# Graph convolution: one-bin tiles in the edge table (500 for 588), and four bin additions a group spread over VectorE's step

## The chip, the cores and the metric

The kernel runs on one core of a Trainium2 chip. The metric is the device time of one execution in microseconds, the median of 3 runs. Engines are named as the profile names them: PE is TensorE (PEld its weight loads), DVE is VectorE, ACT is ScalarE, POOL is GpSimd, SP is SyncE.

## What is computed

A graph of 3750 nodes with 256 features and 60000 edges goes through four layers, each added to its input: a relational attention, a mixture of small experts, a graph convolution (`_L1_gnn_ref`), and a routed mixture of 16 experts. The change concerns the third:

```python
row, col = (ei[0], ei[1])
filt = jax.nn.silu(rbf @ Wf1 + bf1) @ Wf2 + bf2     # rbf: 60000 x 20, Wf1: 20 x 256, Wf2: 256 x 256
msg = x[col] * filt
agg = jax.ops.segment_sum(msg, row, num_segments=x.shape[0])
h = jax.nn.silu(agg @ Wu1 + bu1) @ Wu2 + bu2
# then a batch norm of h over the nodes, and x + bn
```

`row` is the edge's `src` and `col` its `dst`. So for each edge a filter of 256 values is computed from 20 attributes, multiplied by the gathered row of the `dst` node, and summed into the `src` node.

## The kernel before

**Bins and tiles.** The 3750 nodes are 30 bins of 128 (`NT`). Edges are sorted by the bin of the node that they are summed into, and cut into tiles of 128 edges, one edge to a partition. K = 4 tiles make a group. `rank` (L407) computes for each edge its place in the order; it rounds the edges of a bin up to `SIZE = group * P` places. For the table of the convolution (`table1`, records of 24 floats: 20 attributes, the `dst` row, the place of `src` in its bin) `group` is K, so each bin is padded to a multiple of 512 places, and the four tiles of a group belong to one bin. The table has ET = 588 tiles, 147 groups. It is first filled with empty records, whose row number is 0 and whose place is -1 (`fill1`, L1953, in 28 DMAs), then POOL scatters the real records into it beside the attention stage and elsewhere. The bin of each group is in `bins1`. The attention stage has a table of its own, by `dst`, in the same 588 tiles.

**The convolution (`convolve`, L1331)** is one stage between two barriers. SP loads the first 588 tiles of `table1` into SBUF in one DMA (L1384), then the smaller weights. Then all engines walk the same steps t = 0 to 151; in a step each works on groups at different distances behind t (`parts`). Steps 0 to 5 and 147 to 151 are written out, the rest is a loop of three steps. In step t:

- POOL gathers 4 x 128 rows of `xtab` for a group, three slots `got`, released by the messages of the group three earlier (L1399).
- ACT copies attributes to bf16 (L1415), applies silu to the first layer (L1420), moves transposed attributes out of PSUM (L1424).
- PE, in this order: four transposes of the attributes of group t-1 into `pT` (L1439); the first layer of group t-2 into `p1` (L1446); the second layer of group t-3 into `pf[0]` and `pf[1]`, two tiles each (L1454); the sum over the edges of group t-4, four matmuls with the one-hot matrix that accumulate in 256 columns of one of three banks `psum` (L1463).
- DVE, in this order: the number of the bin of group t-5 is read from SBUF into a register (`value_load`, L1481); the one-hot of group t-3 (L1486); three instructions that split the attributes of group t into a high and a low bf16 part, `rest`, copy and low part (L1492, L1494, L1496; the last lets PE transpose that group in the next step); the bias added to both halves of the filter of group t-3 (L1502); both halves of the messages (L1507); `agg[bin] += psum` for group t-5 (L1512).

The semaphores that matter below: `filtered` (PE to DVE, a half of `pf` is done), `filt_ready` and `msg_ready` (DVE, halves of the filter and of the messages), `attr_ready` (DVE to PE, the low part is written), `summed` (PE to DVE), `agg_done` (DVE to PE, the bank may be written again). `filt` has one buffer, `msg`, one-hot, `attr` and `got` have three. In the attention stage DVE reads a bin number in the same way: of its four maxima in a row (L863, each released by PE) the fourth has such a load ahead of it. A matmul with fp32 operands appears in the profile as two records.

```python
if 5 in parts:
    dve.wait_ge(summed, t - 4)
    wait_positive(dve, agg_done, t - 5)
    at = flat(agg[:, bass.ds(bin5, 1), :])
    v.tensor_tensor(at, at, psum[s5][:, 0:D], ALU.add).then_inc(agg_done, 1)
```

## Time and profile before

| what | value |
|---|---|
| median of 3 runs | 4170.98 us (4170.66 to 4171.43) |
| the profiled execution: its time, its span | 4176.44 us, 4174.7 us |
| PE busy | 2928.3 us, 70% of the span |
| DVE busy | 2177.3 us, 52% |
| POOL busy | 2277.2 us, 55% |
| ACT busy | 1210.5 us, 29% |
| the convolution, from its first DMA to its last addition | 2398.2 to 3301.6 us |

The stages follow one another with a barrier between them, so a stage's length goes whole into the total. A share of the whole span is an average over stages with different limits; the stage in question has to be read by itself. "Idle before" in a row names what ended the wait. A row of the timeline with xN merges N instructions that follow each other; their ends overlap the next start a little, so the distance of two starts (the pitch) is shorter than a duration.

### The profile page before, as it was taken

What the parts mean: (1) busy time and instruction counts of PE and PEld (TensorE: products, weight loads), DVE (VectorE), ACT (ScalarE), POOL (GpSimd) and SP (SyncE); (2) the same over time, 40 slices, a digit from 0 to 9 for tenths busy, and PEclk for the clock granted to TensorE, in tenths of its full rate; (3) what the DMA queues carried; (4) which work ended last, traced back from release to release, by engine and by line L of the source; (5) the groups of instructions that cost most, each with busy time, mean ns of one, the idle gap of its engine ahead of it and who ended that gap; (6) DMA issues with size and microseconds to landing.
All of it is one profiled execution on the core that took longest, in us unless ns stands there. A gap on an engine that the chain in (4) does not pass through costs nothing. (4 is left out here: it accounts for less than half of the span.)

```text
span 4174.7 us, 73619 instructions
## 1 busy us (share of the span) xinstructions
PE 2928.3 (70%) x20296; PEld 2364.7 (57%) x20297; DVE 2177.3 (52%) x5961; ACT 1210.5 (29%) x3266; POOL 2277.2 (55%) x2336
## 2 busy tenths in 40 slices
PE   5199101777777777776379679999999864299990
PEld 1188101555555555555255358888888633288990
DVE  8411002877777777777743557777777444011112
ACT  1123000444444444444223223333333231022220
POOL 2777775777777777777240056666666200511115
PEclk8599655998998999999679789999999875599995
DMA  3344101222222222225100143333335501155533
GB/s 105 108 135 137 40 2 32 63 65 63 63 64 63 64 64 63 64 64 62 23 19 1 47 136 89 90 89 90 90 90 84 52 0 39 49 175 173 171 104 114
DMA packets 209214, 317.71 MB, mean 76 GB/s; under 512 B 63367, under 2 KB 150063, under 8 KB 208388
## 3 DMA queue, kind: packets, MB, share of 16 engines
q0 software_dynamic: 95008, 179.89, 19.9%
q1 hardware_dynamic: 103204, 127.24, 9.4%
q10 hardware_dynamic: 10944, 9.97, 0.7%
q8 instruction: 17, 0.28, 0.0%
q14 instruction: 41, 0.34, 0.0%
HBM read 248.03 MB, written 68.84 MB: 76 GB/s over the span
## 5 line engine op out<-in xcount | busy, mean ns | idle before, releaser
L1402 POOL DMA_INDIRECT conv_got<-xtab,conv_rowidx x588 | 565.8, 962 | 313.2 <-DVE conv_msg L1507 156.6
L806 POOL DMA_INDIRECT att_got<-feat,att_rowidx x588 | 573.2, 975 | 201.5 <-issue 150.2
L294 POOL DMA_INDIRECT table<-l0a_rec,l0a_addr x469 | 458.2, 977 | 216.7 <-issue 146.1
L1454 PE MATMUL conv_pf<-conv_wf,conv_act 128*128 128x256 f32 x2352 | 534.0, 380 | 0.2 <-DVE conv_filt L1502 0.2
L812 POOL DMA_INDIRECT table<-recs_rec,recs_addr x432 | 423.2, 980 | 131.6 <-issue 130.4
L1454 PEld LDWEIGHTS conv_pf<-conv_wf,conv_act 128*128 128x128 f32 x2352 | 447.6, 190 | 76.9 <-issue 0.8
L982 PE MATMUL att_pmax<-all_identb,att_away 128*128 128x512 bf16 x588 | 261.1, 444 | 203.9 <-DVE att_elo L901 203.2
L863 DVE TENSOR_REDUCE att_tmax<-att_pmax 128x4 f32<-128x512 f32 x588 | 373.8, 680 | 31.1 <-PE att_pmax L986 27.6
L986 PE MATMUL att_pmax<-all_identb,att_ehi 128*128 128x128 bf16 x2352 | 383.6, 242 | 0.0
L986 PE MATMUL att_pmax<-all_identb,att_elo 128*128 128x128 bf16 x2352 | 383.3, 242 | 0.0
L1420 ACT ACTIVATE conv_act<-conv_p,conv_bf 128x512 f32<-128x512 f32 x294 | 186.2, 684 | 552.1 <-PE conv_p L1446 552.1
L1502 DVE TENSOR_TENSOR conv_filt<-conv_pf,conv_bf 128x512 f32<-128x512 f32 x294 | 202.8, 691 | 222.1 <-PE conv_pf L1454 222.1
L986 PEld LDWEIGHTS att_pmax<-all_identb,att_elo 128*128 128x128 bf16 x2352 | 260.5, 111 | 93.0 <-issue 41.6
L1013 PE MATMUL att_psum<-att_f,att_onehot 128*128 128x260 f32 x1176 | 303.7, 403 | 1.9 <-DVE att_f L925 1.9
L1873 DVE TENSOR_TENSOR moe_hid<-moe_gatev,moe_p 128x512 f32<-128x512 f32 x76 | 52.2, 687 | 484.4 <-ACT moe_gatev L1853 484.4
L1825 PE MATMUL moe_p<-moe_xT,moe_w 128*128 128x128 f32 x2432 | 287.5, 277 | 17.4 <-issue 7.1
L957 ACT ACTIVATE att_f<-att_got,att_ex 128x64 f32<-128x64 f32 x1176 | 294.5, 333 | 0.0
L1825 PEld LDWEIGHTS moe_p<-moe_xT,moe_w 128*128 128x128 f32 x2432 | 278.7, 193 | 23.5 <-issue 18.3
L1463 PE MATMUL conv_psum<-conv_msg,conv_onehot 128*128 128x256 f32 x1176 | 279.0, 380 | 5.6 <-DVE conv_msg L1507 5.6
L1788 POOL DMA_INDIRECT moe_got<-xtab,moe_tokens x76 | 72.0, 948 | 368.2 <-PE moe_pT L1814 358.6
L706 PE MATMUL proj_ps<-proj_w,proj_xs 128*128 128x260 f32 x960 | 220.1, 388 | 74.6 <-DVE proj_wr L652 70.0
L986 PEld LDWEIGHTS att_pmax<-all_identb,att_ehi 128*128 128x128 bf16 x2352 | 260.0, 111 | 0.0
(336 smaller groups left out, 5074.0 us busy)
## 6 DMA issues: line engine op xcount, KB each, us to landing
moe_w<-in_L_ffn_w SPq DMA_DIRECT2D x96, 512.0 KB
feat<-proj_out SPq DMA_DIRECT2D x30, 1040.0 KB
results<-moe_y ACTq DMA_DIRECT2D x76, 128.0 KB, 1.7
att_got<-feat,att_rowidx POOLq DMA_INDIRECT x588
conv_got<-xtab,conv_rowidx POOLq DMA_INDIRECT x588, 2.8
xtab<-ln_row SPq DMA_DIRECT2D x60, 128.0 KB, 1.7
table<-l0a_rec,l0a_addr POOLq DMA_INDIRECT x469
table<-recs_rec,recs_addr POOLq DMA_INDIRECT x469, 2.1
```

What stands on the lines that cost most here:

```text
L294: self.nc.gpsimd.indirect_dma_start(out=self.table, out_offset=bass.IndirectOffsetOnAxis(ap=self.addrs[:, j:j + 1], axis=0), in_=self.recs ...
L806: nc.gpsimd.indirect_dma_start(out=got[g % 3][:, k, :], out_offset=None, in_=feat, in_offset=bass.IndirectOffsetOnAxis(ap=rowidx[:, g * K ...
L812: nc.gpsimd.indirect_dma_start(out=table1, out_offset=bass.IndirectOffsetOnAxis(ap=addr1[:, i:i + 1], axis=0), in_=rec1[:, i, :], in_offse ...
L863: count(v.tensor_reduce(tmax[:, k, :], pmax[k][:, :, :], AX.X, ALU.max))
L957: nc.scalar.activation(f[s2][:, k, h, 0:HD], got[s2][:, k, h * HD:(h + 1) * HD], ACT.Copy, scale=ex[:, k, h:h + 1]).then_inc(last_ready, 1)
L982: nc.tensor.matmul(pmax[k][:, :, :], away[s1][:, k, :], bcast(c["identb"][:, :], [[0, HEADS], [1, P]]), start=True, stop=False, skip_group ...
L986: ins = nc.tensor.matmul(pmax[k][:, h, :], part[s1][:, k, h:h + 1].broadcast_to([P, P]), c["identb"][:, :], start=False, stop=(part is elo ...
L1013: ins = nc.tensor.matmul(psum[:, 0:HEADS * H1], oh[s2][:, k, :], flat(f[s2][:, k, :, :]), start=(k == 0), stop=(k == K - 1))
L1402: nc.gpsimd.indirect_dma_start(out=got[g % 3][:, k, :], out_offset=None, in_=xtab, in_offset=bass.IndirectOffsetOnAxis(ap=rowidx[:, g * K ...
L1454: ins = nc.tensor.matmul(pf[b][:, k, :], act1[s3][:, h, (2 * b + k) * P:(2 * b + k + 1) * P], wf2[:, h, :], start=(h == 0), stop=(h == 1))
L1463: ins = nc.tensor.matmul(psum[s4][:, 0:D], oh[s4][:, k, :], msg[s4][:, k, :], start=(k == 0), stop=(k == K - 1))
L1825: ins = nc.tensor.matmul(ps[w][:, j * P:(j + 1) * P], wt[w][:, k, j * P:(j + 1) * P], xT[w][:, k, :], start=(k == 0), stop=(k == 1))
```

## The change

Three parts. (1) `table1` has tiles of one bin each: `rank` by `src` rounds to 128 places instead of 512, the table has ET1 = 500 tiles (125 groups), and `bins1` holds the bin of each tile. A group of four tiles may now span two bins. (2) Since the four tiles of a group no longer share a bin, PE keeps their sums apart: two tiles write the two halves of one bank, the other two those of the next, and the three banks turn by half groups. (3) DVE adds four sums a group instead of one, each with its own bin number. The additions of group t-5, k = 0 to 3, are spread over the step, and the split of the attributes is spread too. The steps written out at the end are now 7 instead of 5 (the loop takes 123 of 125 groups). The empty records are written in 25 DMAs of 20 tiles instead of 28 of 21.

```diff
+ET1 = 500
+TS1 = ET1 + -(-EJ // P)
...
-TABLE1_PARTS = 28
+TABLE1_PARTS = 25
...
-        rank(nc, "by_src", c, Bins(nc, k, "src", src, src_loaded, 96), NT, ET, TS, addr1[:, :], bins1, K, records1, send)
+        rank(nc, "by_src", c, Bins(nc, k, "src", src, src_loaded, 96), NT, ET1, TS1, addr1[:, :], bins1, 1, records1, send)
...
-    GROUPS, SLOTS = ET // K, 3
+    GROUPS, SLOTS = ET1 // K, 3
...
-            for t in range(GROUPS, GROUPS + 5):
+            for t in range(GROUPS // 3 * 3, GROUPS + 5):
...
-            sp.dma_start(recs[:, :, :], table1.rearrange("(p t) w -> p t w", p=P)[:, 0:ET, :]).then_inc(loaded, 16)
+            sp.dma_start(recs[:, :, :], table1.rearrange("(p t) w -> p t w", p=P)[:, 0:ET1, :]).then_inc(loaded, 16)
...
                     pe.wait_ge(oh_ready, t - 3)
-                    wait_positive(pe, agg_done, t - 6)
-                    for k in range(K):
-                        if k % 2 == 0:
-                            pe.wait_ge(msg_ready, (t - 4) * 2 + k // 2 + 1)
-                        ins = nc.tensor.matmul(psum[s4][:, 0:D], oh[s4][:, k, :], msg[s4][:, k, :], start=(k == 0), stop=(k == K - 1))
-                    ins.then_inc(summed, 1)
+                    for b in two:
+                        wait_positive(pe, agg_done, (t - 4) * K + 2 * b - 4)
+                        pe.wait_ge(msg_ready, (t - 4) * 2 + b + 1)
+                        bank = psum[((u - 4) * 2 + b) % 3]
+                        for k in two:
+                            ins = nc.tensor.matmul(bank[:, k * D:(k + 1) * D], oh[s4][:, 2 * b + k, :], msg[s4][:, 2 * b + k, :], start=True, stop=True)
+                        ins.then_inc(summed, 1)
...
+                def load_bin():
+
+                    if 5 in parts:
+                        bins.append(dve.value_load(bins1[0:1, bass.ds(g5 * K + len(bins), 1)], min_val=0, max_val=NT - 1))
+
+                def add_sum(k):
+                    if 5 in parts:
+                        dve.wait_ge(summed, g5 * 2 + k // 2 + 1)
+                        wait_positive(dve, agg_done, g5 * K + k)
+                        at = flat(agg[:, bass.ds(bins[k], 1), :])
+                        v.tensor_tensor(at, at, psum[((u - 5) * 2 + k // 2) % 3][:, (k % 2) * D:(k % 2 + 1) * D], ALU.add).then_inc(agg_done, 1)
...
+                load_bin()
+                add_sum(0)
                 if 3 in parts:
...
+                load_bin()
+                add_sum(1)
                 if 0 in parts:
...
+                    count(v.tensor_tensor(rest[:, :, :], recs[:, bass.ds(g0 * K, K), 0:NG], attr[u][:, :, 0, 0, :], ALU.subtract))
+                filters(0)
+                load_bin()
+                add_sum(2)
+                messages(0)
+                load_bin()
+                if 0 in parts:
                     count.wait()
                     count(v.tensor_copy(attr[u][:, :, 0:2, 1, :], rest[:, :, :].unsqueeze(2).broadcast_to([P, K, 2, NG])))
+                add_sum(3)
+                filters(1)
+                if 0 in parts:
                     count.wait()
                     v.tensor_tensor(attr[u][:, :, 2, 1, :], rest[:, :, :], attr[u][:, :, 0, 1, :], ALU.subtract).then_inc(attr_ready, 1)
...
+                messages(1)
```

The new helpers `filters(b)` and `messages(b)` are the old lines for one half, with the same waits.

How the instructions lie now. On DVE in the loop, before the change, from the first filter half to the next step's one-hot (names: `conv_filt` the filter with its bias, `conv_msg` the messages, `l2b_agg` the sums by bin; TENSOR_LOAD reads the bin number, REGISTER_ALU and ISA are arithmetic on registers and waits):

```order
L1502 TENSOR_TENSOR conv_filt<-conv_pf0,conv_bf2 128x512
L1500 REGISTER_ALU
L1502 TENSOR_TENSOR conv_filt<-conv_pf1,conv_bf2 128x512
L1507 TENSOR_TENSOR conv_msg1<-conv_filt,conv_got1 128x512 x2
L1512 ISA
L1512 TENSOR_TENSOR l2b_agg<-l2b_agg,conv_psum2 128x256
L1481 REGISTER_ALU
L1481 TENSOR_LOAD all_bins1
L1481 ISA x2
L1486 ISA
L1486 TENSOR_TENSOR conv_onehot2<-all_ramp,conv_recs 128x512
```

Here both filter halves follow each other directly, and the only load of a bin number stands between the last addition and the next one-hot; that addition is the one that is replaced by four. After the change, the same engine from the first filter half to the third addition:

```order
L1504 TENSOR_TENSOR conv_filt<-conv_pf0,conv_bf2 128x512
L1490 ISA
L1490 TENSOR_LOAD all_bins1
L1490 ISA x2
L1494 REGISTER_ALU
L1497 ISA
L1497 TENSOR_TENSOR l2b_agg<-l2b_agg,conv_psum2 128x256
```

The second addition now stands ahead of the filter, and the third directly behind its first half, with a load and a wait between. And on from there, up to the low part of the attributes (`conv_attr`), which PE waits for:

```order
L1512 TENSOR_TENSOR conv_msg1<-conv_filt,conv_got1 128x512
L1490 ISA
L1490 TENSOR_LOAD all_bins1
L1490 ISA x2
L120 ISA
L1534 CAST conv_attr1<-conv_rest 128x4x2x20
L1497 ISA
L1497 TENSOR_TENSOR l2b_agg<-l2b_agg,conv_psum2 128x256
L1501 REGISTER_ALU
L1504 TENSOR_TENSOR conv_filt<-conv_pf1,conv_bf2 128x512
L120 REGISTER_ALU
L1539 TENSOR_TENSOR conv_attr1<-conv_rest,conv_attr1 128x4x20
```

Two additions and two loads of a bin number have come in between the first filter half and the low part of the attributes, and the low part itself, which stood ahead of both filter halves, now stands behind both.

On PE in the loop, before, from the second half of the first layer to the sum over a group's edges:

```order
L1454 MATMUL conv_pf0<-conv_wf2,conv_act11 128x256 x4
L1454 MATMUL conv_pf1<-conv_wf2,conv_act11 128x256 x4
L117 REGISTER_ALU
L1463 MATMUL conv_psum0<-conv_msg0,conv_onehot0 128x256 x4
L1436 REGISTER_ALU
L1439 MATMUL conv_pT<-all_identb,conv_attr1 120x128 x4
```

One wait's register precedes the four matmuls into one bank, which now are two pairs; after the change:

```order
L1457 MATMUL conv_pf0<-conv_wf2,conv_act11 128x256 x4
L1457 MATMUL conv_pf1<-conv_wf2,conv_act11 128x256 x4
L120 ISA
L1467 MATMUL conv_psum0<-conv_msg0,conv_onehot0 128x256 x2
L120 REGISTER_ALU
L1467 MATMUL conv_psum1<-conv_msg0,conv_onehot0 128x256 x2
```

The sum of a group has the same four matmuls, now two into each of two banks, with arithmetic for a wait between them; nothing else of PE's step has moved.

## Rows read from the trace of the kernel before

**Rows 1.** View of busy time by stretch, PEclk the granted clock, one 100 us stretch:

```profile
2600.00:2700.00 100.00, 100.00 (x515) 85.79 (x515) 72.31 (x154) 34.91 (x69) 65.70 (x70) 1.00 0.37 90
```

**Rows 2.** Waits in 2460 to 3280 us: total us, times, longest:

```profile
DVE conv_filt L1502 <- PE conv_pf L1454: 212.7, 274, 1.0
```

**Rows 3.** Timeline, PE, one step: start, us, work, xcount, [idle before]:

```profile
2901.05 0.39 PE L1439 MATMUL conv_pT<-all_identb,conv_attr 128*120 128x128 bf16 x4
...
2901.71 3.62 PE L1454 MATMUL conv_pf<-conv_wf,conv_act 128*128 128x256 f32 x16
2905.17 1.89 PE L1463 MATMUL conv_psum<-conv_msg,conv_onehot 128*128 128x256 f32 x8
2906.89 0.39 PE L1439 MATMUL conv_pT<-all_identb,conv_attr 128*120 128x128 bf16 x4
```

**Rows 4.** Timeline, DVE, the same step:

```profile
2901.34 0.41 DVE L1512 TENSOR_TENSOR l2b_agg<-l2b_agg,conv_psum 128x256 f32 x1
2901.67 0.74 DVE L1486 TENSOR_TENSOR conv_onehot<-all_ramp,conv_recs 128x512 f32<-128x512 f32 x1
2902.34 0.23 DVE L1492 TENSOR_TENSOR conv_rest<-conv_recs,conv_attr 128x80 f32<-128x80 bf16 x1
2902.60 0.24 DVE L1494 CAST conv_attr<-conv_rest 128x160 bf16<-128x160 f32 x1
2902.88 0.24 DVE L1496 TENSOR_TENSOR conv_attr<-conv_rest,conv_attr 128x80 bf16<-128x80 f32 x1
2903.64 0.69 DVE L1502 TENSOR_TENSOR conv_filt<-conv_pf,conv_bf 128x512 f32<-128x512 f32 x1 [0.52 <-PE conv_pf L1454]
2905.37 0.69 DVE L1502 TENSOR_TENSOR conv_filt<-conv_pf,conv_bf 128x512 f32<-128x512 f32 x1 [1.03 <-PE conv_pf L1454]
2905.97 1.28 DVE L1507 TENSOR_TENSOR conv_msg<-conv_filt,conv_got 128x512 f32<-128x512 f32 x2
2907.18 0.41 DVE L1512 TENSOR_TENSOR l2b_agg<-l2b_agg,conv_psum 128x256 f32 x1
```

**Rows 5.** Timeline, PE weight loads, the same step:

```profile
2906.68 0.46 PEld L1439 LDWEIGHTS conv_pT<-all_identb,conv_attr 128*120 128x120 bf16 x4
```

**Rows 6.** Timeline of the attention stage, DVE and PE:

```profile
1203.52 1.49 DVE L863 TENSOR_REDUCE att_tmax<-att_pmax 128x4 f32<-128x512 f32 x2 [0.32 <-PE att_pmax L986]
...
1208.84 0.17 DVE L901 TENSOR_TENSOR att_elo<-att_e,att_ehi 128x16 bf16<-128x16 f32 x1
...
1209.07 0.10 PEld L982 LDWEIGHTS att_pmax<-all_identb,att_away 128*128 128x128 bf16 x1 [1.22 <-DVE att_elo L901]
1209.07 0.39 PE L982 MATMUL att_pmax<-all_identb,att_away 128*128 128x512 bf16 x1 [1.13 <-DVE att_elo L901]
...
1211.20 2.47 DVE L863 TENSOR_REDUCE att_tmax<-att_pmax 128x4 f32<-128x512 f32 x4
```

**Rows 7.** Groups by line, POOL in 2460 to 3280 us:

```profile
L1402 POOL DMA_INDIRECT conv_got<-xtab,conv_rowidx x560 | 537.8, 960 | 282.7 <-DVE conv_msg L1507 151.3 <-issue 131.3
```

**Rows 8.** Timeline at the start of the convolution:

```profile
2398.54 0.35 SPq L1384 DMA_DIRECT2D conv_recs<-table  x1
...
2419.32 0.28 DVE L1472 CAST conv_wparts<-conv_wf 20x256 bf16<-20x256 f32 x1 [23.56 <-DMA conv_bf<-in_L_gnn_bf]
```

**Rows 9.** Timeline at the end of the convolution:

```profile
3251.28 0.69 DVE L1507 TENSOR_TENSOR conv_msg<-conv_filt,conv_got 128x512 f32<-128x512 f32 x1 [0.74 <-DMA conv_got<-xtab,conv_rowidx]
...
3278.84 1.89 PE L1463 MATMUL conv_psum<-conv_msg,conv_onehot 128*128 128x256 f32 x8
...
3297.20 1.29 DVE L1507 TENSOR_TENSOR conv_msg<-conv_filt,conv_got 128x512 f32<-128x512 f32 x2 [3.01 <-DMA conv_got<-xtab,conv_rowidx]
3298.41 0.41 DVE L1512 TENSOR_TENSOR l2b_agg<-l2b_agg,conv_psum 128x256 f32 x1
3299.04 0.42 DVE L1512 TENSOR_TENSOR l2b_agg<-l2b_agg,conv_psum 128x256 f32 x1 [0.21 <-DVE l2b_agg L1512]
3301.15 0.42 DVE L1512 TENSOR_TENSOR l2b_agg<-l2b_agg,conv_psum 128x256 f32 x1 [1.69 <-PE conv_psum L1463]
```

More of the change, by code:

```diff
@@ L26 @@
 TS = ET + -(-EJ // P)
+ET1 = 500
+TS1 = ET1 + -(-EJ // P)
+assert (EDGES + NT * (P - 1)) // P <= ET1 and ET1 % K == 0
 assert 0 < EV <= EJ and (EDGES + NT * (K * P - 1)) // (K * P) <= ET // K and ET % (3 * K) == 0
@@ L1482, in step, with messages @@
+                def messages(b):
+                    if 3 in parts:
+                        if b == 0:
+                            dve.wait_ge(got_s[s3], i * 16 * K)
+                        dve.wait_ge(filt_ready, g3 * 2 + b + 1)
+                        part = slice(2 * b, 2 * b + 2)
+                        v.tensor_tensor(msg[s3][:, part, :], filt[:, part, :], got[s3][:, part, :], ALU.mult).then_inc(msg_ready, 1)
+                load_bin()
+                add_sum(0)
                 if 3 in parts:
-                    g = t - 3
@@ L1488, in step @@
                 if 0 in parts:
-                    count = Steps(dve, dv, t * 2)
-                    dve.wait_ge(h_ready, t + 1)
-                    wait_positive(dve, attr_ready, t)
-                    count(v.tensor_tensor(rest[:, :, :], recs[:, bass.ds(t * K, K), 0:NG], attr[u][:, :, 0, 0, :], ALU.subtract))
+                    dve.wait_ge(h_ready, g0 + 1)
+                    wait_positive(dve, attr_ready, g0)
+                    count(v.tensor_tensor(rest[:, :, :], recs[:, bass.ds(g0 * K, K), 0:NG], attr[u][:, :, 0, 0, :], ALU.subtract))
```

42 lines of the change are left out of this document (16 added, 26 removed).

## The prediction

> **What bounds the kernel now.** The views were read from the outside in: busy time by stretch, waits, then the timeline of one step on each engine. In the convolution's loop PE is busy for 100.00 of 100 us at a granted clock of 1.00, the upper of its two levels (2.4 GHz), while DVE is busy 72.3 us [rows 1]. What the reader is to see there: not a gap on PE, and 28% of slack on DVE. The waits say the same: DVE waits for PE ahead of the filter, 212.7 us in all, with never more than 1.0 us at a time [rows 2]. So a step is as long as PE's matmuls in it, 3.46 us for the second layer, 1.72 us for the sum, 0.66 us for transposes and first layer together [rows 3]. From the sum that starts at 2905.17 to the one at 3278.84 there are 64 steps [rows 3, 9], (3278.84 - 2905.17) / 64 = 5.84 us each. Time can leave this stage by fewer steps, or at its two ends.
>
> **The sum.** It is made against the profiled execution, 4176.4 us, which lies 5.4 us above the median of 4171.0; the difference is carried over.
>
> *Fewer groups.* 147 groups become 125, and the loop counts are fixed in the code, so 22 steps go whatever the data are. PE has the same matmuls in a group as before, of the same shapes, so if it stays without a gap a step stays 5.84 us: 22 x 5.84 = 128.5 us less. A gain beyond that within a step is excluded, because PE already has no idle time [rows 1].
>
> *Three more additions on DVE.* From start to start an addition takes 0.33 us, a one-hot 0.67, `rest` 0.26, the copy 0.28, the low part 0.24, each half of filter or messages 0.60 [rows 4]; together 0.33 + 0.67 + 0.26 + 0.28 + 0.24 + 4 x 0.60 = 4.18 us. With three additions more it is 5.17 us of 5.84. In total DVE has room. Two of the four stand ahead of the filter, where DVE waits 0.52 us even now and where the old order had the copy and the low part too [rows 4].
>
> *The low part behind the second filter half.* This is the tight place, so it is followed instruction by instruction. PE begins each step with the transposes of the attributes whose low part DVE wrote in the step before; everything else of PE is queued behind that wait. Before, the low part was done at 2903.12, 3.8 us ahead of the transpose at 2906.89 [rows 3, 4]. Now it comes last in a chain that only starts when PE releases the first filter half, at 2903.64 in the step shown: filter half 0.60, addition 0.33, message half 0.60, copy 0.16 (0.24 less the 0.08 by which neighbours overlap when they need not wait for each other, as 0.41 against 0.33 shows), addition 0.33, second filter half 0.60, low part 0.24: 2.86 us. DVE to PE takes 0.06 us more: `att_elo` ends at 1208.84 + 0.17 = 1209.01 and PE starts at 1209.07 [rows 6]. Sum 2.92 us. PE begins to load the transpose's weights, which are these attributes, at 2906.68, and starts the matmul at 2906.89 [rows 3, 5]; that leaves 3.04 us and 3.25 us. So it arrives 0.12 us early.
>
> *The loads of a bin number.* There are four a step instead of one, and two lie in this chain. The trace before shows the same load between the third and fourth of the four maxima in the attention stage. Where DVE's data are there, the four run in 2.47 us, which is 3 x 0.60 + 0.68: the load costs nothing. Where the third has just been released by PE, it and the fourth take 1.49 us, so they start 0.81 us apart and not 0.60 [rows 6]. So a load behind a released instruction costs between 0 and 0.21 us, and that is how the third addition stands behind the first filter half. I take the 0.21 us once, as the nearest row: the chain is 3.13 us. The weight load would be 0.09 us late, the matmul still 0.12 us early, and the two can begin together, as both do at 1209.07 [rows 6]. The later loads lie behind work of 0.60 us that is already queued. I count no stall. If instead none of the seven overlapped its neighbour, the chain would be 0.69 + 0.41 + 0.68 + 0.24 + 0.41 + 0.69 + 0.24 + 0.21 + 0.06 = 3.63 us, 0.38 us late. So the price of this edit lies between 0 and 0.38 us a step, and I take 0, from the chain whose pitches are measured in the same loop. The Trainium skill, "DMA: Bandwidth & Descriptors", section on latency and other measured facts, gives a floor of about 600 ns for a `tensor_load`; no run here times one by itself. By that rule, with the loads uncovered, the sum would be that of the last rival below; the row of 2.47 us says that at least the covered load is free.
>
> *Other waits that the change adds.* Half of a bank of PSUM is rewritten three half groups later instead of three groups: the second half of PE's sum needs the first two additions of DVE's same step. The two follow the last message half, so they end about 1.8 us into PE's step, and are needed at 4.12 + 0.86 = 5.0 us (the sum starts 4.12 us after the transposes) [rows 3]. Additions of one group wait for each other, but each has another instruction of 0.6 us or a load between. POOL issues four gathers a group, (537.8 + 131.3) / 140 = 4.8 us of 5.84 with what it spends between them [rows 7], and its release, the end of the second message half, stays where it was within 0.2 us. All of this: 0.
>
> *The table's load.* The stage starts with one load of 588 tiles, asked for at 2398.54; DVE begins at 2419.32 [rows 8]. 15% fewer bytes of 20.8 us is at most 3.1 us; with about 2 us of fixed latency left out it is 2.7 us less. Its lower bound is 0. The fill with empty records, in 25 pieces for 28, ran beside DVE and PE work in a stage that ends 30 us later: 0. The sort, group size aside, has the same instructions: 0.
>
> *The end.* Counted from the edges that the reference draws, sorted by source they fill 131 of the 147 groups of 512, and will fill 482 of the 500 tiles of 128. The rest are empty records which all gather row 0. Those gathers are slow: the message of the ninth empty group is the first that waits for its DMA, 0.74 us, and the last one waits 3.01 us [rows 9]. After the change there are only four and a half empty groups, so no message should wait. Without these waits the sum of group 143 at 3278.84 would be followed by that of 144 at 3284.7, of 145 at 3289.9 (no transposes and no first layer any more) and of 146 at 3291.6, ending at 3293.4. The last addition ended at 3301.15 + 0.42 = 3301.57. Behind the last sum there are now up to three chained additions, 0.63 us apart as two are at 3298.41 and 3299.04 [rows 9], some 1.5 us: end at 3294.9, 6.7 us less. Bounds 0 and 8 us.
>
> Together 128.5 + 2.7 + 6.7 = 137.9 us. Profiled 4176.4 - 137.9 = 4038.5 us; median 4171.0 - 137.9, rounded 4033 us. With the two small terms at their bounds, 4031 to 4042.
>
> **The rivals.** *A stall at the transposes.* PE waits for the low part in each of the 120 steps in which all engines take part. For it: a margin of 0.12 us that stands on seven pitches. Against it: every pitch comes from this loop. Between 0 and 0.38 us a step it costs 0 to 46 us; at the middle, 0.19 us, 4033 + 23 = 4056 us.
>
> *DVE becomes the bound through the loads, and the kernel gets slower.* If each of four loads holds up the engine, the step becomes 5.17 us plus four times that. It decides from the step at which all gains are spent: 137.9 / 125 = 1.10 us above 5.84, that is 6.94 us, or 0.44 us a load. The rows bound an uncovered load at 0.60 us, the pitch that hides it. Then the step is 7.57 us, (7.57 - 5.84) x 125 = 216 us are added, and the median is 4249 us. Against it: the 0.21 us above, and the old loop, where a load stands between addition and one-hot and these still start 0.33 us apart [rows 4]. That the change doesn't do what it says is not open here: the number of steps is written in the code.
>
> **How the numbers follow.** The forecast has 0.72, the stall 0.24, the slower case 0.04. A measurement of this kernel tells about 0.2%, 8 us, from no change; both first cases are far beyond that. Faster 0.95, same 0.01, slower 0.04. The range takes the forecast's own bounds, 3 us below for what the pieces of the start could give in addition, and two thirds of the stall's: 4028 to 4064 us.
>
> **What would show it.** Right: in the profile after, PE still busy 100 of 100 us in the loop at clock 1.00; 5.84 us from sum to sum; DVE busy near 5.2 us a step; the low part ending 0.1 to 0.4 us before the transposes; no wait of the last messages for their gathers; the first DVE instruction 2 to 3 us sooner behind the table's load. Wrong: "idle before" on the transposes, put down to the low part, tells of the stall and its size; gaps on DVE in front of the additions that no engine releases ("issue") tell of the loads; a sum whose second half waits for an addition tells that the banks are too few.

## The result, and the profile after

The changed kernel takes 4070.2 us (median of 4 runs, 4066.9 to 4075.8). The ratio to the kernel before is 0.976, 95% interval 0.9743 to 0.9777: faster by 2.4%. Forecast were 4033 us with a range of 4028 to 4064, so the sign is right, three quarters of the gain are there, and the time lies 6 us outside the range.

| stretch of the two profiled executions | before | after | difference | forecast |
|---|---|---|---|---|
| up to the request for the table | 2398.5 | 2393.3 | -5.3 | 0 |
| from there to the first VectorE instruction | 20.8 | 18.1 | -2.7 | -2.7 |
| from there to the end of the last addition | 882.25 | 780.40 | -101.85 | -128.5 - 6.7 |
| all that follows (with what lies outside the span) | 874.9 | 876.7 | +1.8 | 0 |
| time of the profiled execution | 4176.4 | 4068.4 | -108.0 | -137.9 |

The miss is in the third row: 33 us of the convolution's gain are missing. Of the two outer rows, in code that the change barely touches, 3.5 us of gain come in addition, which no run explains. And the execution profiled before lay 5.4 us above its median, the one after 1.8 us below: 7 us of the miss in the median are not in the sum at all.

The start of the convolution, timelines of SP and DVE after, answers to [rows 8]:

```profile
2393.26 0.35 SPq L1387 DMA_DIRECT2D conv_recs<-table  x1
...
2411.32 0.28 DVE L1476 CAST conv_wparts<-conv_wf 20x256 bf16<-20x256 f32 x1 [20.83 <-DMA conv_bf<-in_L_gnn_bf]
```

Busy time by stretch after, in the order PE, PEld, DVE, ACT, POOL, then PEclk, DMA share, GB/s; against [rows 1]:

```profile
2600.00:2700.00 100.00, 98.91 (x497) 80.88 (x496) 86.15 (x199) 32.69 (x64) 63.36 (x66) 1.00 0.30 87
```

The clock is at its upper level as before, so PE's matmuls are not slower. But PE now has 1.1 us of gaps in 100, and its matmuls, 515 before, are 497, 3.5% fewer. The gaps that the view shows are the smaller part of the loss, because the durations in the rows of PE run over the next start: from the sum to the transposes it was 1.72 us before [rows 3] and is 2.10 us below (2904.84 to 2906.94), of which the view shows 0.21 as idle. The waits of the stage after, 2460 to 3180 us (total us, times, longest), against [rows 2]:

```profile
DVE l2b_agg L1497 <- issue: 79.6, 231, 0.7
PEld conv_pT L1442 <- DVE conv_attr L1539: 37.2, 77, 0.6
...
DVE conv_filt L1504 <- PE conv_pf L1457: 9.2, 42, 0.6
PE conv_pT L1442 <- DVE conv_attr L1539: 8.2, 38, 0.2
```

The roles have turned. DVE's wait for PE ahead of the filter has shrunk from 212.7 to 9.2 us; PE and its weight loads wait for the low part of the attributes instead. And ahead of the additions DVE has 79.6 us of idle time that no engine ends ("issue"). One step of PE, timeline after, against [rows 3]:

```profile
2900.68 0.43 PE L1442 MATMUL conv_pT<-all_identb,conv_attr 128*120 128x128 bf16 x4
...
2901.39 3.62 PE L1457 MATMUL conv_pf<-conv_wf,conv_act 128*128 128x256 f32 x16
2904.84 1.89 PE L1467 MATMUL conv_psum<-conv_msg,conv_onehot 128*128 128x256 f32 x8
2906.94 0.43 PE L1442 MATMUL conv_pT<-all_identb,conv_attr 128*120 128x128 bf16 x4 [0.21 <-DVE conv_attr L1539]
...
3144.44 0.43 PE L1442 MATMUL conv_pT<-all_identb,conv_attr 128*120 128x128 bf16 x4 [0.21 <-DVE conv_attr L1539]
```

From 2906.94 to 3144.44 there are 39 steps: 6.09 us each, 0.25 more than 5.84. Three steps make one turn of the loop and differ (6.26, 6.00, 6.00); the one shown is that of 6.26, in which DVE comes around the loop. And DVE's timeline of the same step after, against [rows 4]:

```profile
2900.46 0.69 DVE L1512 TENSOR_TENSOR conv_msg<-conv_filt,conv_got 128x512 f32<-128x512 f32 x1
2901.86 0.42 DVE L1497 TENSOR_TENSOR l2b_agg<-l2b_agg,conv_psum 128x256 f32 x1 [0.71 <-issue]
2902.20 0.68 DVE L1519 TENSOR_TENSOR conv_onehot<-all_ramp,conv_recs 128x512 f32<-128x512 f32 x1
2902.97 0.42 DVE L1497 TENSOR_TENSOR l2b_agg<-l2b_agg,conv_psum 128x256 f32 x1
2903.31 0.23 DVE L1526 TENSOR_TENSOR conv_rest<-conv_recs,conv_attr 128x80 f32<-128x80 bf16 x1
2903.48 0.69 DVE L1504 TENSOR_TENSOR conv_filt<-conv_pf,conv_bf 128x512 f32<-128x512 f32 x1
2904.47 0.42 DVE L1497 TENSOR_TENSOR l2b_agg<-l2b_agg,conv_psum 128x256 f32 x1 [0.30 <-issue]
2904.81 0.68 DVE L1512 TENSOR_TENSOR conv_msg<-conv_filt,conv_got 128x512 f32<-128x512 f32 x1
2905.50 0.24 DVE L1534 CAST conv_attr<-conv_rest 128x160 bf16<-128x160 f32 x1
2905.71 0.42 DVE L1497 TENSOR_TENSOR l2b_agg<-l2b_agg,conv_psum 128x256 f32 x1
2906.05 0.68 DVE L1504 TENSOR_TENSOR conv_filt<-conv_pf,conv_bf 128x512 f32<-128x512 f32 x1
2906.65 0.23 DVE L1539 TENSOR_TENSOR conv_attr<-conv_rest,conv_attr 128x80 bf16<-128x80 f32 x1
```

Each addition with a load ahead of it starts late. Behind the last message half it is 1.40 us where the loop turns, and 0.90 or 1.00 in the two other steps (0.60 assumed), behind the one-hot 0.77 (0.67), behind the first filter half 0.99 (0.60 and once 0.21). The end of the stage, DVE's timeline after, against [rows 9]:

```profile
3185.11 0.42 DVE L1497 TENSOR_TENSOR l2b_agg<-l2b_agg,conv_psum 128x256 f32 x1
3185.95 0.42 DVE L1497 TENSOR_TENSOR l2b_agg<-l2b_agg,conv_psum 128x256 f32 x1 [0.41 <-PE conv_psum L1467]
...
3191.30 0.42 DVE L1497 TENSOR_TENSOR l2b_agg<-l2b_agg,conv_psum 128x256 f32 x1 [0.78 <-DVE l2b_agg L1497]
```

The additions here stand 0.83 us apart and not 0.63. No message waits for its gather any more, as forecast.

The views count only instructions that move data. The trace also records DVE's register instructions, and between the first filter half and the addition behind it they read so (start us, duration us, operation, line):

```
2903.479 0.691 TENSOR_TENSOR   L1504  conv_filt<-conv_pf,conv_bf
2903.504 0.057 FUSED_REGOPS    L1490  address of the bin number
2903.595 0.303 TENSOR_LOAD     L1490
2903.933 0.190 FUSED_REGOPS    L1490  range check
2904.157 0.023 SEQ_ASSERT      L1490  range check
2904.214 0.040 ALU_OP          L1494
2904.301 0.021 EVENT_SEMAPHORE L120   wait for the addition before
2904.370 0.057 FUSED_REGOPS    L1497  wait for PE's sum, address
2904.474 0.422 TENSOR_TENSOR   L1497  l2b_agg<-l2b_agg,conv_psum
```

This is 0.97 us of register work, with the spaces between its pieces. It begins only when the filter half has started, so the addition follows that start by 0.99 us where the filter half covers 0.60; 0.39 us are not covered. That reading is the theory to test, and within it there are two: the load itself, or the range check behind it (0.28 us from 2903.933 to 2904.214). The same records say why the turn of the loop is worse: ahead of the load stand the loop's branch and its register arithmetic (L1378), 0.30 us from the branch at 2900.518 to the arithmetic at 2900.816, so the load's record starts at 2900.956, 0.49 us behind the start of the message half, where it is 0.09 us in the next step (2906.893 behind 2906.801).

### The profile page after: what moved, and what is told of

Read it like the earlier page. It is cut to its first block and busy times, and to the rows that moved or that the text cites. A ratio compares the mean times of both kernels' runs of the same rounds, so it can differ in the third digit from the quotient of the medians.

```text
span 4066.7 us, 74150 instructions
## 1 busy us (share of the span) xinstructions
PE 2815.2 (69%) x19636; PEld 2243.9 (55%) x19637; DVE 2209.5 (54%) x6138; ACT 1164.8 (29%) x3178; POOL 2191.5 (54%) x2248
## 5 line engine op out<-in xcount | busy, mean ns | idle before, releaser
L1405 POOL DMA_INDIRECT conv_got<-xtab,conv_rowidx x500 | 483.3, 967 | 290.8 <-DVE conv_msg L1512 160.0
L1457 PE MATMUL conv_pf<-conv_wf,conv_act 128*128 128x256 f32 x2000 | 454.2, 380 | 0.0
L1457 PEld LDWEIGHTS conv_pf<-conv_wf,conv_act 128*128 128x128 f32 x2000 | 380.7, 190 | 65.2 <-issue 0.3
L1423 ACT ACTIVATE conv_act<-conv_p,conv_bf 128x512 f32<-128x512 f32 x250 | 158.2, 684 | 499.3 <-PE conv_p L1449 499.3
L1853 PEld LDWEIGHTS moe_p<-moe_xT,moe_w 128*128 128x128 f32 x2432 | 279.1, 193 | 23.7 <-issue 23.6
L1497 DVE TENSOR_TENSOR l2b_agg<-l2b_agg,conv_psum 128x256 f32 x500 | 210.6, 421 | 97.2 <-issue 81.2
L996 PE MATMUL att_pT<-all_identb,att_away 128*128 128x128 bf16 x588 | 59.4, 226 | 270.1 <-ACT att_away L953 270.1
```

The source lines that it names most:

```text
L1405: nc.gpsimd.indirect_dma_start(out=got[g % 3][:, k, :], out_offset=None, in_=xtab, in_offset=bass.IndirectOffsetOnAxis(ap=rowidx[:, g * K ...
L1457: ins = nc.tensor.matmul(pf[b][:, k, :], act1[s3][:, h, (2 * b + k) * P:(2 * b + k + 1) * P], wf2[:, h, :], start=(h == 0), stop=(h == 1))
L1853: ins = nc.tensor.matmul(ps[w][:, j * P:(j + 1) * P], wt[w][:, k, j * P:(j + 1) * P], xT[w][:, k, :], start=(k == 0), stop=(k == 1))
```

## The experiments

Times are medians with lowest and highest; ratios are to the kernel before, run on the same chip. "Steps" are the 113 middle distances between the starts of PE's transposes in the profiled execution. "Checks" are the checks of a loaded value's range.

### Are the loads the cause, and what do they cost?

Kernel before on this chip: 4168.1 us (4164.6 to 4170.2).

**No loads at all.** The bins are the constants 0 to 3, so the sums by bin are not computed, with all additions in their place.

```diff
-                        bins.append(dve.value_load(bins1[0:1, bass.ds(g5 * K + len(bins), 1)], min_val=0, max_val=NT - 1))
+                        bins.append(len(bins))
```

> The changed kernel without its four loads of a bin number in a step; the four additions go to the fixed bins 0 to 3, so the sums by bin are not computed, everything else is as in the changed kernel, waits included. Loads theory (DVE issues too slowly because each load holds up what follows): an addition starts 0.60 to 0.65 us behind the first filter half instead of 1.00, the step falls from 6.09 to 5.84 us, the time by about 0.25 x 117 = 29 us plus 2 to 4 us at the end, to 4035 to 4042 us. Waits theory (the separate waits and register arithmetic ahead of each addition cost it): the 1.00 us stays, the time stays at 4060 to 4076. Order theory (the low part behind both filter halves is late for the transposes): PE still waits for the low part, the step stays above 6.0 us, the time at 4060 to 4076.

Measured: 4034.0 us (4029.7 to 4036.8), ratio 0.9679 (0.9663 to 0.9695); all steps 5.84 us. Timeline of DVE in this kernel:

```profile
2903.12 0.69 DVE L1504 TENSOR_TENSOR conv_filt<-conv_pf,conv_bf 128x512 f32<-128x512 f32 x1 [0.97 <-PE conv_pf L1457]
2903.73 0.41 DVE L1497 TENSOR_TENSOR l2b_agg<-l2b_agg,conv_psum 128x256 f32<-128x256 f32 x1
```

The addition stands 0.61 us behind the filter half, and DVE waits for PE again. The loads with what belongs to them (check, address, and here one separate wait too) are the whole loss of the step; without them the three additions, the new order and the banks cost nothing.

**Eight more loads in the kernel before**, at the head of each step, to measure the price by itself.

```diff
+                    for _ in range(EXTRA):
+                        dve.value_load(bins1[0:1, bass.ds(t - 5, 1)], min_val=0, max_val=NT - 1)
```

> The kernel before with eight further loads of the same bin number at the head of each of its 152 steps, their values unused: it measures a load by itself. Loads theory: the sum of addition with load takes 0.82 us in the steps written out after the change and 0.42 of it without, so a load with its two checks costs 0.4 to 0.8 us; eight take 3.2 to 6.4 us, DVE's step has 1.6 us of slack and the step grows to 7 to 11 us, the time by 180 to 700 us. If a load is nearly free (the reading of the prediction), the step stays 5.84 us and the time within 5 us of the kernel before.

Measured once: 4606.8 us. Timeline of DVE in this kernel:

```profile
2902.86 0.41 DVE L1515 TENSOR_TENSOR l2b_agg<-l2b_agg,conv_psum 128x256 f32 x1
2908.21 0.69 DVE L1489 TENSOR_TENSOR conv_onehot<-all_ramp,conv_recs 128x512 f32<-128x512 f32 x1 [4.94 <-PE conv_psum L1464]
```

Between the starts of the addition and of the one-hot lie 5.35 us. In the trace's records the nine loads start 0.61 us apart (median of the distances), from 2902.488 to 2907.429, each followed by its check; the address is worked out once. So a load with its check takes 0.61 us. Both this and the mean step of 8.8 us are as the loads theory expected. The releaser named in the row has long been done: the time is register work, which the view does not show.

**The split of the attributes ahead of both filter halves**, as in the kernel before.

```diff
+                if 0 in parts:
+                    count.wait()
+                    count(v.tensor_copy(attr[u][:, :, 0:2, 1, :], rest[:, :, :].unsqueeze(2).broadcast_to([P, K, 2, NG])))
+                    count.wait()
+                    v.tensor_tensor(attr[u][:, :, 2, 1, :], rest[:, :, :], attr[u][:, :, 0, 1, :], ALU.subtract).then_inc(attr_ready, 1)
                 filters(0)
...
                 load_bin()
-                if 0 in parts:
...
                 add_sum(3)
                 filters(1)
-                if 0 in parts:
...
                 messages(1)
```

> The changed kernel with the split of the attributes (copy and low part) put back ahead of both filter halves, all loads and additions as changed. Order theory: the transposes no longer wait, the step falls to 5.84 us, the time to 4035 to 4042 us. Loads theory: DVE issues as much as before, so the step stays 6.0 to 6.1 us and the time 4058 to 4076 us; only the wait of PE changes its name, from the low part to a filter half.

Measured: 4109.6 us (4105.3 to 4111.1), ratio 0.9858 (0.9841 to 0.9874), mean step 6.47 us. It is 39 us slower than the change and outside both expectations. Waits of this kernel, 2460 to 3180 us:

```profile
DVE l2b_agg L1497 <- issue: 72.8, 184, 0.8
PEld conv_pf L1457 <- DVE conv_filt L1504: 67.6, 110, 0.7
```

PE hardly waits for the low part any more (7.2 us of its weight loads), but for the filter, which must have read a bank before PE writes it again, and the weight loads of its sums wait 23.6 us for additions. The place where PE waits is therefore not the cause: DVE is late as a whole, and PE meets it at the first thing that it needs. Why this order is slower than the change was not tested by a run; a likely reason is that the short copy and low part between the halves also cover register work, and moved out cover none.

**One load of four registers** at the head of the step instead of four loads; all eight bounds are still checked.

```diff
-                    if 5 in parts:
-                        bins.append(dve.value_load(bins1[0:1, bass.ds(g5 * K + len(bins), 1)], min_val=0, max_val=NT - 1))
+                    if 5 in parts and not bins:
+                        _, values = nc.values_load_multi_w_load_instructions(bins1[0:1, bass.ds(g5 * K, K)],
+                            engines=[mybir.EngineType.DVE], min_val=0, max_val=NT - 1)
+                        bins.extend(values)
```

> The changed kernel with one load of four registers at the head of each step instead of four loads of one; the range checks (two a number) stay, all eight behind the load. Loads theory: the addition behind the first filter half starts 0.6 to 0.7 us after it, the wait ahead of the first addition of the step grows to 0.5 to 1.2 us; in all DVE needs less than before, the step lies between 5.84 and 6.0 us, the time at 4037 to 4058 us. Waits theory and order theory: 4060 to 4076.

Measured: 4080.2 us (4076.9 to 4081.0), ratio 0.9791 (0.9775 to 0.9807), mean step 6.21 us: 10 us slower than the change where it was expected to be faster. Timeline of DVE in this kernel:

```profile
2904.27 0.68 DVE L1514 TENSOR_TENSOR conv_msg<-conv_filt,conv_got 128x512 f32<-128x512 f32 x1
2906.54 0.42 DVE L1499 TENSOR_TENSOR l2b_agg<-l2b_agg,conv_psum 128x256 f32 x1 [1.60 <-issue]
```

In the trace's records the load of four takes 0.344 us against 0.302 for one (medians of 125 and 500), and each register's check 0.27 to 0.28 us more, 1.1 us for four. Three loads saved are 0.9 us of register work, and still the kernel is slower: all checks stand in one bunch, of which one instruction covers 0.6 us. The row shown is at the turn of the loop, where the branch adds to it. That made the check a suspect of its own.

### Load or check, and the place

The values are limited to NT - 1 where `rank` makes them, so the check can be left out. The first variant keeps four loads, the second is one load of four at the head of the step, the third has one load with its checks behind the one-hot, the fourth one load without checks behind the one-hot.

```diff
-                        bins.append(dve.value_load(bins1[0:1, bass.ds(g5 * K + len(bins), 1)], min_val=0, max_val=NT - 1))
+                        _, values = nc.values_load_multi_w_load_instructions(bins1[0:1, bass.ds(g5 * K + len(bins), 1)],
+                            engines=[mybir.EngineType.DVE], min_val=0, max_val=NT - 1,
+                            skip_runtime_bounds_check_because="rank limits every entry to NT - 1")
+                        bins.extend(values)
```

and for the place, in the third and fourth:

```diff
-                load_bin()
-                add_sum(0)
                 if 3 in parts:
...
                 load_bin()
+                add_sum(0)
                 add_sum(1)
```

In the second to fourth only the first call of `load_bin` in a step loads, and it loads all four.

> The changed kernel with its four loads of a bin number left where they are, but without the range checks behind them. Theory A (the load itself is the cost: VectorE's queue can't pass it, the checks ride along): the pitches of 0.9 to 1.0 us at the later additions stay within 0.1 us, the step stays at 6.0 to 6.1 us, the time at 4060 to 4073. Theory B (the checks are a large part, a third or more of the 0.59 us that a load with its checks took at the head of a step): a load costs 0.35 us or less, it fits behind a 0.60 us addition, the step falls to 5.84 to 5.90 us, the time to 4034 to 4048.

> The changed kernel with one load of four registers at the head of the step and no range checks. Against the form with one load and eight checks in a bunch (gap of 1.2 to 1.6 us ahead of the first addition, 4080). Theory A (the load is the cost, the checks are nearly free): the gap stays above 1.0 us, the time at 4065 to 4080. Theory B (the checks are the cost): the gap falls to 0.8 us or less, all later additions stand at pitches of 0.60 us, the step falls to 5.84 to 5.95 us, the time to 4034 to 4052.

> One load of four registers with its eight checks, but behind the one-hot instead of ahead of it, so that the transposes, which wait for the one-hot, no longer wait for the load. Theory A (the cost is VectorE's time: the queue is stopped for 1.2 to 1.6 us a step wherever the load stands, and VectorE has about 1.3 us of slack in a step of 5.84): the step stays at 6.0 to 6.3 us, the time at 4060 to 4080. Theory B (the cost is where it stands: only a stop ahead of the one-hot holds the transposes back): the wait of the weight load of the transposes on the one-hot goes, the step falls to 5.84 to 5.95 us, the time to 4034 to 4052.

> Both at once: one load of four registers, no range checks, behind the one-hot. If either the checks or the place is the cause, TensorE sets the step again: 5.84 us, VectorE waits for the filter product once a step as in the kernel before, the time is 4030 to 4045, within 10 us of the kernel without any load (4034). If the load itself is the whole cost and VectorE's time the bound, the step stays at 6.0 us or more and the time at 4060 or more.

Measured: 5201, 5172, 5148 and 5190 us, beside 5272 us (5236 to 5315) for the kernel before. This chip is another, 26% slower with the same program, and all four missed every expected time. Its loss begins ahead of the first gather, behind the scatters into the attention's table: that gather is issued at 951 us, on the first chip at 704. In the convolution 55 to 64 of the 113 steps are over 7 us. On another such chip (the next section) the waits of the kernel with four bare loads, 3430 to 4280 us, hold a line that the first chip's traces do not have:

```profile
DVE conv_filt L1507 <- DMA xtab<-ln_row: 115.6, 33, 4.5
```

The view puts up to 4.5 us of DVE's waiting down to a DMA, named after the one that wrote `xtab`, the table from which the gathers read; that it is late gathers is likely and not shown. Totals that hang on this cannot rank variants 1% apart. What can be read are the steps that it leaves alone, and they already part the theories: between 5.80 and 5.90 us lie 37 steps of four bare loads, 46 of one bare load at the head, 48 of one bare load behind the one-hot, and 24 of the one load with checks behind the one-hot, which has 18 more up to 6.0 and 14 between 6.2 and 6.3.

### The same on another chip

> The changed kernel itself, beside the variants on one chip. On a chip whose gathers do not disturb the stage it repeats: ratio to the kernel before 0.976, 4066 to 4076, steps of 5.95 to 6.27 us. On a chip that lands the gathers late (as the one that ran the first four variants without checks did, with steps of 7 to 10 us in more than half the stage) every variant loses the same and none can be ranked.

> The changed kernel without range checks, four loads, on another chip than the first time. There 37 of its 113 steps, those without a late gather, were 5.80 to 5.90 us, and none of the changed kernel's are. Theory B (the checks are what makes the stall, the bare load fits): nearly all steps at 5.84 to 5.90 us, ratio 0.967 to 0.970, 4030 to 4044. Theory A (the load is the cost, and those short steps only used slack that a late gather before them had left): steps of 5.95 to 6.2 us, ratio 0.973 to 0.976.

> One load of four with its eight checks, behind the one-hot, on another chip than the first time. If only the place counts: 5.84 us, ratio below 0.970. If VectorE's time is the bound (busy 5.2 us of a step, 1.8 us stopped at the load and its checks): 6.0 to 6.2 us, ratio 0.974 to 0.980.

> One load of four, no checks, behind the one-hot, on another chip than the first time. TensorE sets every step, 5.84 us, ratio 0.967 to 0.969, 4029 to 4038; the end of the stage, where additions no longer wait for loads either, within 1 us of the kernel without loads. It is as fast as the form with four bare loads if four bare loads already fit, and up to 10 us faster if they fit only just.

Measured: 5130 (5120 to 5138), 5169 (5150 to 5189), 5155 and 5160 us beside 5273 us (5243 to 5307) for the kernel before: a chip like the last. The steps read the same way. The changed kernel has none below 5.90 us (60 between 5.9 and 6.1, 17 between 6.2 and 6.3), four bare loads have 49 at 5.80 to 5.90, one bare load behind the one-hot 53, and one load with checks behind the one-hot 5, with 51 between 5.9 and 6.0. The totals say otherwise: here four bare loads are 39 us slower than the change, with ranges that do not touch, and in the profiled executions 62 of 113 steps are over 7 us against 34. So on such a chip no gain from taking the checks out is seen, and that every variant loses the same there, as was expected, is not borne out; why was not studied. Still open was whether the short steps only used slack that a late gather had left ahead of them.

### On a chip like the first

Kernel before: 4171.2 us (4166.1 to 4176.3).

> The changed kernel once more beside two variants, in case this chip lands the gathers in time as the one of the very first runs did (kernel before near 4170): then 4066 to 4076 and steps of 5.95 to 6.27 us. Near 5270 for the kernel before, the gathers set more than half the stage again and the totals rank nothing.

> Four bare loads, no range checks, on a chip without late gathers: steps of 5.84 us throughout, as in the 49 undisturbed ones of the last run, ratio 0.967 to 0.970, 4030 to 4044. If those steps only used slack that late gathers left behind: 5.95 us or more, ratio 0.973 to 0.976.

> One load of four without checks behind the one-hot, on a chip without late gathers: steps of 5.84 us, ratio 0.967 to 0.969, 4029 to 4038, at most 6 us below the form with four bare loads, from the last steps of the stage alone, where additions follow each other without TensorE between them.

| kernel | us | ratio | steps |
|---|---|---|---|
| the change | 4067.9 (4067.2 to 4070.7) | 0.9751 (0.9735 to 0.9767) | 6.00 to 6.29 |
| four loads, no checks | 4034.7 (4032.4 to 4037.6) | 0.9670 (0.9654 to 0.9686) | 5.84 |
| one load, no checks, behind the one-hot | 4036.7 (4036.3 to 4037.7) | 0.9678 (0.9662 to 0.9694) | 5.84 |

All three as the theory of the checks expected. Leaving out the checks gives 33.2 us and reaches the kernel without any load (4034.0): four bare loads a step cost nothing here. Without checks the place and the number of loads no longer matter. Either is enough, then: to take away loads and checks together, or the checks alone. What is too long is the row of register instructions as a whole; that a check by itself does more harm than a load of the same length is not shown. Busy time by stretch, four loads without checks:

```profile
2600.00:2700.00 100.00, 100.00 (x515) 85.76 (x514) 86.61 (x207) 34.73 (x68) 65.13 (x69) 1.00 0.32 90
```

Its waits, 2460 to 3180 us:

```profile
DVE conv_filt L1507 <- PE conv_pf L1457: 73.3, 119, 1.1
...
DVE l2b_agg L1500 <- issue: 17.0, 39, 0.5
```

Its timeline of DVE in one step:

```profile
2902.66 0.69 DVE L1507 TENSOR_TENSOR conv_filt<-conv_pf,conv_bf 128x512 f32<-128x512 f32 x1 [0.29 <-PE conv_pf L1457]
2903.36 0.42 DVE L1500 TENSOR_TENSOR l2b_agg<-l2b_agg,conv_psum 128x256 f32 x1
2903.70 0.68 DVE L1515 TENSOR_TENSOR conv_msg<-conv_filt,conv_got 128x512 f32<-128x512 f32 x1
2904.30 0.24 DVE L1537 CAST conv_attr<-conv_rest 128x160 bf16<-128x160 f32 x1
2904.45 0.41 DVE L1500 TENSOR_TENSOR l2b_agg<-l2b_agg,conv_psum 128x256 f32 x1
2904.78 0.69 DVE L1507 TENSOR_TENSOR conv_filt<-conv_pf,conv_bf 128x512 f32<-128x512 f32 x1
2905.39 0.23 DVE L1542 TENSOR_TENSOR conv_attr<-conv_rest,conv_attr 128x80 bf16<-128x80 f32 x1
```

PE is without a gap again, and DVE waits for PE in each of the 119 steps. The addition stands 0.70 us behind the filter half against 0.99 with the check, the difference of 0.29 us being the check's 0.28. It also shows that the bare load is not quite covered where the filter half has just been released: 0.10 us over 0.60. The last additions, DVE's timeline at the end of this kernel's stage, stand 0.63 us apart:

```profile
3156.03 0.42 DVE L1500 TENSOR_TENSOR l2b_agg<-l2b_agg,conv_psum 128x256 f32 x1
3156.66 0.42 DVE L1500 TENSOR_TENSOR l2b_agg<-l2b_agg,conv_psum 128x256 f32 x1 [0.21 <-DVE l2b_agg L1500]
...
3160.46 0.42 DVE L1500 TENSOR_TENSOR l2b_agg<-l2b_agg,conv_psum 128x256 f32 x1 [0.21 <-DVE l2b_agg L1500]
```

### The checks in attention, and the place once more

The first variant leaves out the checks in the attention stage as well (VectorE L841, TensorE L998), in the same way; the second is the one load with checks behind the one-hot.

> The form with four bare loads in the convolution, and in the attention stage, too, the range checks behind the loads of a bin number are left out (two a step on VectorE, one on TensorE, 147 steps). If the checks cost time wherever VectorE is released late: 0.27 us for each of one to two loads a step, 40 to 80 us less than the form with checks in attention, 3955 to 3995. If attention is paced by its gathers (VectorE waits up to 4.3 us a step for them, 146 us in 1000 to 2000 us of the trace), that wait grows by what the checks leave and the time stays within 8 us of 4035. I take the second.

> One load of four registers with its eight checks, behind the one-hot, this time on a chip that lands its gathers in time. If only the place counts: 5.84 us a step, 4034 to 4045. If VectorE's time is what is short: 5.9 to 6.1 us a step (the undisturbed ones on the last chip were mostly 5.9 to 6.0), 4045 to 4065, between the changed kernel (4068 to 4070) and the one without checks (4035).

Measured: 5100 us (5093 to 5149) and 5143 us (5119 to 5171) beside 5233 us (5223 to 5262) for the kernel before, again a chip of the slower kind. No expected time can be judged there. The second has 31 steps at 5.80 to 5.90 us and 17 more up to 6.1. Both questions stay open: whether moving a checked load behind the one-hot is worth a part of the 33 us, and whether the checks cost anything in attention.

## Why the prediction was wrong

- **Fewer groups, -128.5 us: right.** With the checks gone the 125 groups run at 5.84 us, and from the first filter's `rest` to the last addition the stage takes 745.7 us against 879.8 before, 134.1 us less; forecast for the loop and the end together were 135.2.
- **Three more additions on DVE, 0: right** by the kernel without loads and by the one without checks.
- **The low part behind the second filter half, 0: right as an order, wrong as an outcome.** Without checks the chain from the start of the first filter half to the end of the low part is 2905.39 + 0.23 - 2902.66 = 2.96 us, where the rows gave 2.86. The tight place was rightly named. In the change the same chain takes 2906.65 + 0.23 - 2903.48 = 3.40 us in the step shown.
- **The loads of a bin number, 0 of a range from 0 to 0.38 us a step: the step that failed**, in its words "The later loads lie behind work of 0.60 us that is already queued. I count no stall". In these places the work ahead is not lined up: behind an instruction that still waits for PE, or for another result of DVE, the register instructions start only when that one does, and a load with its check, two waits and an address then takes 0.97 us. Measured are 0.25 us a step, about 117 times, 29 us; the mean lay inside the bounds, and the value was taken from the wrong end. Of the 0.54 us that the chain has over the 2.86 of the rows, 0.39 stand at the load behind the first filter half, counted at 0.21, and 0.14 at the next one, counted at 0 (0.69 and 0.21 us from message half to copy to addition, for 0.60 and 0.16). In the step of 6.26 us the whole can be read off: the filter half starts 2.80 us behind the transposes (2903.48 - 2900.68) where it was 2.59 before [rows 3, 4], because the two additions ahead of it, which the prediction had put into DVE's slack, now come late through their own loads and the turn of the loop; and the chain from there ends 0.21 us after PE could have started (3.40 + 0.06 against 3.25). Together 0.42 us, more than the 0.38 taken as the upper bound. The nearest row, 0.21 us behind a released maximum in attention, was of the right kind, but that instruction has one wait and no address from the register behind its load; here it was 0.39 us. And in the row of 2.47 us for four maxima the trace's records show the load's register work start at 1211.28 and the load at 1211.35, over 1.0 us ahead of the third maximum (1212.40): with the data there and nothing else to do the register side had run far ahead. In the convolution's step waits stand in between.
- **Other waits, 0: right.** Between 2460 and 3180 us no sum of PE waits for an addition in the change.
- **The table's load, -2.7: right** (-2.7). The working as it stands, 15% of what is left of 20.8 us without 2 us, gives 2.8; that some 2 us of it are fixed no run here shows.
- **The end, -6.7: half right.** The waits of the last messages are gone. But with checks the chained additions take 0.83 us each, and the last eight starts lie 6.2 us apart (3185.11 to 3191.30) where without checks they lie 4.4 us apart (3156.03 to 3160.46). The working also gave group 144 a full step of 5.84 us behind 143, though no transposes are left in it; that is a few tenths of a microsecond.
- **Median and profile.** The forecast carried the 5.4 us between profiled execution and median over. They did not carry over: the medians of the change are 4070.2 and 4067.9, its profiled execution 4068.4.
- **The rivals.** The stall at the transposes was priced at 4033 to 4079 with 4056 in the middle, and it is what the profile shows, with the loads as its cause. It got 0.24 and only two thirds of its length in the range; the whole of it would have held the time. The slower case needed DVE held up 0.44 us by each load; its idle time ahead of the additions is 79.6 us in some 120 steps, about 0.17 us a load, and since DVE had slack the step grew by only 0.06 for each.

The range was too narrow for a reason that could be seen: the margin that was left, 0.12 us, was smaller than the one price, 0.21 us, that had to be taken at the nearest row.

## What to carry to other kernels

Where an engine's instruction takes its address from a value that is loaded in the loop, count the register instructions between it and the one ahead (load, check, waits, address), each with its space, and compare the sum with the duration of that one instruction: what is longer is a stall, and the busy share of the engine does not show it. Idle time that no engine ends, put down to "issue", in front of such instructions is its sign. A loop's branch belongs in the sum as well. A range check that the data make needless is worth leaving out where the engine has little slack; on a chip that runs the kernel before in 4171 us the checks cost 33 us where the change gained 101, and on a slower chip the kernel without them showed no gain (5169 us against 5130).

## What the runs showed of the hardware

- On DVE a load of one register from SBUF takes 0.30 us in the trace's records (500 of them), of four registers at once 0.344 us (125). The Trainium skill, "DMA: Bandwidth & Descriptors", section "Latency and other measured facts", gives about 600 ns as the floor of a `tensor_load`: the record is half of it, and 0.61 us is what a load takes together with its check in a row of nine. The Trainium skill, "Runtime: NRT & Kernel Launch", section "Instruction fetch mechanics", has some 200 ns for each register, of loads from HBM; of these no run here shows any, and from SBUF each further register cost 0.014 us.
- The check of one value's range, two more instructions, takes 0.27 to 0.28 us, nearly as much as the load.
- DVE's register instructions run beside those that move data, but not past one that still waits. In the kernel with four bare loads the first filter half waits for PE in 117 steps (0.6 us in the mean, 1.1 at most), and the register work behind it starts 0.013 to 0.015 us after it, never sooner. In the change's step above it starts 0.025 us after it (2903.504); the register work for the load of the next step starts at 2906.78, where the second message half gets the filter half that it waits for (2906.051 + 0.683 gives 2906.73) and itself starts at 2906.80. From there 0.60 us are covered. Without such a wait they were 1.1 us ahead, in the attention stage.
- Where DVE comes around its loop, 0.30 us pass from the start of the branch (a record of 0.056 us) to the next register instruction, in each of 39 turns.
- Of the five chips of the experiments three ran the same kernel in 5233 to 5273 us and the other two in 4168 and 4171. On the three, steps of the changed kernel and its variants go up to 10 us, and single waits of DVE that the view puts down to a DMA are up to 6.7 us long (in the changed kernel). What makes those chips late was not studied.
